# Region and embedding gathers in overlapping fours, and a reordered set-up, in a two-layer LSTM kernel

## What is computed

```python
rp = jnp.concatenate([region_tbl[region_idx], poi_tbl[poi_idx]], -1)
nv = jnp.concatenate([rp @ W_rp + b_rp, coords @ W_co + b_co], -1)
conv = jax.nn.elu(lax.conv_general_dilated(nv, conv_w, (1,), 'VALID', ...) + conv_b)
emb = jnp.tanh(jnp.concatenate([car_tbl[car_idx], week_tbl[week_idx], time_tbl[time_idx]], -1))
x = jnp.concatenate([conv, jnp.broadcast_to(emb[:, None, :], conv.shape[:2] + (27,))], -1)
h = _lstm_layer(x, Wih0, Whh0, bih0, bhh0)
h = _lstm_layer(h, Wih1, Whh1, bih1, bhh1)
return ((h[:, -1, :] @ W1 + b1) @ W2 + b2) @ W3 + b3
```

## Time and profile before

| | |
|---|---|
| median of 3 runs | 1105.63 us (1104.09 to 1105.67) |
| profiled execution | 1107.28 us, its span 1105.5 us |
| mean granted TensorE clock | 0.991 |
| PE busy | 1071.1 us (97%) |
| DVE busy | 741.9 us (67%) |
| ACT busy | 511.5 us (46%) |
| POOL busy | 319.6 us (29%) |
| HBM read, written | 11.21 MB, 4.19 MB |

### The profile page before, as it was taken

One profiled execution on the slowest core, in us unless ns is written; L12 is line 12 of the kernel. 1 busy time (PEld: TensorE's weight loads), 2 busy tenths in 40 slices (PEclk: granted clock), 3 DMA queues, 4 the chain that ended last, 5 costly groups with the idle time before them and its releaser, 6 DMA issues.

```text
span 1105.5 us, 14346 instructions
## 1 busy us (share of the span) xinstructions
PE 1071.1 (97%) x4898; PEld 515.5 (47%) x4898; DVE 741.9 (67%) x1146; ACT 511.5 (46%) x737; POOL 319.6 (29%) x339
## 2 busy tenths in 40 slices
PE   5879999999999999999999999999999999999998
PEld 4654444444445444444444444444444544444444
DVE  3667766657777757567676858666686768766553
ACT  1354554444554544444554544444455544444432
POOL 3563045552440034552450025562541000000000
PEclk8979999999999999999999999999999999999999
DMA  9611001000010101000010101000010101000001
GB/s 240 135 14 16 1 3 31 2 2 1 2 31 2 39 3 31 3 2 1 2 31 1 41 2 31 3 2 1 2 31 1 39 1 27 3 0 1 1 1 38
DMA packets 36808, 22.57 MB, mean 20 GB/s; under 512 B 25303, under 2 KB 29447, under 8 KB 36615
## 3 DMA queue, kind: packets, MB, share of 16 engines
q1 hardware_dynamic: 24432, 20.53, 6.8%
q0 software_dynamic: 9984, 1.12, 2.6%
q10 hardware_dynamic: 2327, 0.08, 0.2%
HBM read 11.21 MB, written 4.19 MB: 14 GB/s over the span
## 4 chain that ended last, share of the span: by engine, by line
PE 85%; DVE 5%; issue 3%; DMA 2%; SPq 2%; ACT 2%; POOL 1%; DVEq 0%; ACTq 0%; POOLq 0%
PE acc L1311 49%; PE acc L1302 25%; PE acc L1293 5%; SPq L428 2%; PE aux L1400 2%; DMA feat<-in_L_rec_region_tbl,region_idx 2%; PE acc L1222 1%; POOL feat L549 1%; DVE neg_part L971 1%; PE aux L1163 1%; ACT gates L727 1%; PE aux L1257 1%; DVE h_full L1046 1%; DVE h_part L1047 1%; DVE gates L999 1%
## 5 line engine op out<-in xcount | busy, mean ns | idle before, releaser
L1311 PE MATMUL acc<-h_part,wh 128*128 128x512 f16 (+1 forms) x2688 | 656.0, 380 | 1.6 <-DVE h_part L1050 1.6
L1311 PEld LDWEIGHTS acc<-h_part,wh 128*128 128x128 f16 x2688 | 245.2, 98 | 321.6 <-issue 54.9
L1302 PE MATMUL acc<-h_part,wh 128*128 128x512 f16 (+1 forms) x1488 | 358.5, 379 | 0.0
L727 ACT ACTIVATE gates<-acc,gate_bias,unscale 128x512 f32<-128x512 f32 x254 | 195.9, 777 | 317.9 <-PE acc L1311 279.5
L727 ACT ACTIVATE gates<-gates,gate_bias,unscale 128x512 f32<-128x512 f32 x242 | 189.9, 811 | 152.4 <-DVE gates L999 142.4
L1302 PEld LDWEIGHTS acc<-h_part,wh 128*128 128x128 f16 x1488 | 144.5, 98 | 177.4 <-issue 6.2
L549 POOL DMA_INDIRECT feat<-in_L_rec_region_tbl,region_idx x160 | 161.9, 1012 | 182.8 <-PE acc L1311 127.7
L999 DVE TENSOR_TENSOR gates<-acc,emb_gates 128x512 f32<-128x512 f32 x242 | 161.3, 686 | 53.5 <-PE acc L1311 45.5
L549 POOL DMA_INDIRECT feat<-in_L_rec_poi_tbl,poi_idx x120 | 120.2, 1002 | 117.2 <-PE acc L1311 99.6
L1293 PE MATMUL acc<-x_in,wx 96*128 96x512 f32 (+1 forms) x248 | 137.3, 560 | 7.3 <-DMA x_in<-conv_hi 4.8
L1046 DVE TENSOR_TENSOR h_full<-gates,tanh_c 128x512 f32<-128x512 f32 x120 | 82.6, 689 | 75.8 <-ACT tanh_c L732 71.2
(11 more groups left out here) (135 smaller groups left out, 358.5 us busy)
## 6 DMA issues: line engine op xcount, KB each, us to landing
out<-y SPq DMA_DIRECT2D x16, 256.0 KB, 2.1
x_in<-conv_hi SPq DMA_DIRECT2D x56, 64.0 KB
feat<-in_L_rec_region_tbl,region_idx POOLq DMA_INDIRECT x160
w<-in_L_rec_W SPq DMA_DIRECT2D x2, 1024.0 KB, 9.3
w_nat<-in_L_rec_Whh SPq DMA_DIRECT2D x2, 1024.0 KB
w<-in_L_rec_W SPq DMA_DIRECT2D x1, 2048.0 KB
feat<-in_L_rec_poi_tbl,poi_idx POOLq DMA_INDIRECT x120
x_in<-conv_lo SPq DMA_DIRECT2D x28, 64.0 KB
```

The source lines that it names most:

```text
L727: nc.scalar.activation(gates[layer][:, j, g, :], source, ACT.Tanh if g == GATE_G else ACT.Sigmoid, bias=gate_bias[:, layer, m:m + 1], scal ...
L1302: mm = nc.tensor.matmul(bank, wh[:, 1, a, c, rows], h_part[0][:, s.write_slot, b, c, :], start=(c == 0 and a == b == HI), stop=(s.first an ...
L1311: mm = nc.tensor.matmul(bank, wh[:, own_w, a, c, rows], h_part[layer][:, s.read_slot, b, c, :], start=False, stop=(c == HK - 1 and a == LO))
```

## The change

- **Gathers of chunk 0.** POOL starts as soon as the small indices are there with the embeddings' first four (car and time for two groups), then step 0's region four; the embeddings' second four once the first has landed; step 1 once step 0 has landed; step 2 once the second embedding four has; step 3 once step 1 has. Two semaphores (`rows_first_in[0]`, `[1]`) are used in turn. At most eight gathers are under way. The copy of the embeddings follows at once. The coordinates of chunk 0 are copied by ACT (`coords_first_put`).
- **Loads.** Whh0 comes before `poi_all`, which is loaded in eight pieces (`POI_PIECES`); W3 comes after Wih1 and Whh1; the week table goes to ACT's queue. The biases and b2 are loaded as rows of 128 (`bias_nat`, ACT's queue), transposed by PE (`turn_biases`) and added by DVE out of `aux` (`add_biases`).
- **Order.** PE multiplies the first four blocks of W1 W2 ahead of the projection's transpose and the band; `turn_wh(2)` and the embeddings' gates come before the first cell; the second half of `product_head` comes between the first and the second cell. DVE looks up the week first, makes the one-hot after the scales, and `row_maxima(1)` after `put_wx_lo`. The head's bias is summed in one piece between the fourth and the fifth cell, into a bank of `aux`, and `b_head` is made after the fifth cell.
- **Loop.** The first three cells of a chunk's body, (1,0), (0,2) and (1,1), stand at the end of the body before it (`early_cells`), and for chunk 0 in the set-up. Their order is the same.
- **Embeddings.** ACT writes `emb_in` with a second Tanh from the source, instead of DVE copying it.

```diff
+POI_PIECES = 4
...
-    return first, second
+    return (first, second) + early_cells(base, steps - 1)
+
+
+def early_cells(base, last_t):
+
+    bank = 14 % 4
+    return (make_cell(base, 1, 0, bank, (0, base.tile(2)), last_t),
+            make_cell(base, 0, 2, (bank + 6) % 4, (1, base.tile(1)), last_t),
+            make_cell(base, 1, 1, (bank + 6) % 4, (0, base.tile(3)), last_t))
...
-        bank = 14 % 4
-        yield cell(base, 1, 0, bank, (0, base.tile(2)))
-        bank = (bank + 6) % 4
-        yield cell(base, 0, 2, bank, (1, base.tile(1)))
-        yield cell(base, 1, 1, bank, (0, base.tile(3)))
+        bank = (14 + 6) % 4
...
+        if following:
+            for early in early_cells(after, last_t):
+                yield "cell", early
...
-        WH_BANKS = ((0, 1, 2, 1), (2, 1, 0, 3), (3, 1, 0, 2))
+        WH_BANKS = ((0, 1, 2, 1), (2, 0, 1, 3), (2, 0, 1, 3))
...
+            load(w_nat[0][:, :, :], d["Whh0"].rearrange("(m p) k -> p m k", p=P), w_in[0])
+
             poi_rows_of = d["r_poi_idx"][0:NCOL, :].rearrange("(s b) t -> s (b t)", s=SIDES)
+            piece = NCOL // SIDES * T // POI_PIECES
             for side in range(SIDES):
-                load(poi_all[side * POI:(side + 1) * POI, :, :].rearrange("k b t -> k (b t)"),
-                     poi_rows_of[side:side + 1, :].partition_broadcast(POI)[:, 0, :], poi_all_in)
-            load(w_nat[0][:, :, :], d["Whh0"].rearrange("(m p) k -> p m k", p=P), w_in[0])
+                for i in range(POI_PIECES):
+                    cols = slice(i * piece, (i + 1) * piece)
+                    load(poi_all[side * POI:(side + 1) * POI, :, :].rearrange("k b t -> k (b t)")[:, cols],
+                         poi_rows_of[side:side + 1, cols].partition_broadcast(POI)[:, 0, :], poi_all_in)
             load(wx_nat[:, :, 0:D_X], d["Wih0"].rearrange("(m p) k -> p m k", p=P), wx_in)
             coord_rows = d["r_coords"].rearrange("(g p) t c -> p g (t c)", p=P)
             load(coords[:, 0:GR, :], coord_rows[:, 0:GR, :], coords_in)
-            load(week_tbl[:, :, :].rearrange("p w d -> p (w d)"),
-                 d["week_tbl"].rearrange("(a w) d -> a (w d)", a=1).partition_broadcast(P)[:, 0, :], week_tbl_in)
-            load(w3[:, :, :], d["W3"].rearrange("(k p) n -> p k n", p=P), w3_in)
-            for layer in range(2):
-                for i, k in enumerate(("bih", "bhh")):
-                    load(bias_in[:, layer, i, :], d[f"{k}{layer}"].rearrange("(m p) -> p m", p=P), bias_loaded)
             for i, k in ((1, "Wih1"), (2, "Whh1")):
                 load(w_nat[i][:, :, :], d[k].rearrange("(m p) k -> p m k", p=P), w_in[i])
+            load(w3[:, :, :], d["W3"].rearrange("(k p) n -> p k n", p=P), w3_in)
...
+                    pool.wait_ge(small_put, 1)
+                    gather_emb(0, 2)
                     pool.wait_ge(idx_ready, 1)
-                    for t in range(PAIR_WIN):
-                        gather_steps(t, t + 1, False, rows_first_in)
-                        pool.wait_ge(rows_first_in, (t + 1) * GR * DMA)
-                    pool.wait_ge(coords_in, DMA)
-                    copy_coords()
-                    pool.wait_ge(small_put, 1)
-                    for g in range(0, GR, 2):
-                        gather_emb(g, g + 2)
-                        pool.wait_ge(emb_rows_in, (g + 2) * (2 * DMA))
+                    gather_steps(0, 1, False, rows_first_in[0])
+                    pool.wait_ge(emb_rows_in, 2 * 2 * DMA)
+                    gather_emb(2, 4)
+                    pool.wait_ge(rows_first_in[0], GR * DMA)
+                    gather_steps(1, 2, False, rows_first_in[1])
+                    pool.wait_ge(emb_rows_in, 4 * 2 * DMA)
+                    gather_steps(2, 3, False, rows_first_in[0])
+                    pool.wait_ge(rows_first_in[1], GR * DMA)
+                    gather_steps(3, 4, False, rows_first_in[1])
...
-            load(b2_col[:, :], d["b2"].rearrange("(k p) -> p k", p=P), b2_in)
+            load(week_tbl[:, :, :].rearrange("p w d -> p (w d)"),
+                 d["week_tbl"].rearrange("(a w) d -> a (w d)", a=1).partition_broadcast(P)[:, 0, :], week_tbl_in)
+            for layer in range(2):
+                for i, k in enumerate(("bih", "bhh")):
+                    row = (layer * 2 + i) * M
+                    load(bias_nat[row:row + M, :], d[f"{k}{layer}"].rearrange("(m p) -> m p", p=P), bias_loaded)
+            load(bias_nat[4 * M:BIASES, :], d["b2"].rearrange("(k p) -> k p", p=P), bias_loaded)
...
+                nc.scalar.activation(emb_in[:, :], source, ACT.Tanh).then_inc(emb_step, 1)
...
+            for m in range(4):
+                put_w12(m)
             put_proj()
-            for m in range(K2):
+            for m in range(4, K2):
                 put_w12(m)
             act.wait_ge(wx_in, DMA)
             for k, first_col, copies, width in ((0, 0, 3, D_CONV), (3, D_CONV, 4, D_EMB)):
                 nc.scalar.copy(wx_rep[:, :, k:k + copies, 0:width],
                                wx_nat[:, :, first_col:first_col + width].unsqueeze(2)
                                .to_broadcast([P, M, copies, width])).then_inc(wx_copied, 1)
+            act.wait_ge(coords_in, DMA)
+            nc.scalar.copy(feat[:, :, :, D_REG + D_POI:D_FEAT],
+                           coords[:, 0:GR, :].rearrange("p g (t c) -> p g t c", c=2)).then_inc(coords_first_put, 1)
...
-            put_head_hi(1)
             emb_tanhs(0, acc[:, 0, :])
             put_wh_hi(1)
-            act.wait_ge(bias_ready, 1)
-            first, second = opening_cells(STEPS)
-            cell_acts(first)
+            put_wh_hi(2)
             for part in range(3):
                 put_emb_gates(0, part)
-            put_wh_hi(2)
+            act.wait_ge(bias_ready, 1)
+            first, *others = opening_cells(STEPS)
+            cell_acts(first)
             put_turned(feat_t[0:KP, 1, :], acc[0:KP, 0, :], turned[0], 1, turned_put[0])
+            put_head_hi(1)
             elu_parts(1, slice(0, HALF))
-            cell_acts(second)
+            for s in others:
+                cell_acts(s)
...
+            def add_biases():
+                dve.wait_ge(bias_turned, 1)
+                bias = aux[:, 3, 0:4 * M].rearrange("p (l i m) -> p l i m", l=2, i=2)
+                nc.vector.tensor_copy(gate_bias[:, :, :], bias[:, :, 0, :]).then_inc(bias_step, 1)
+                nc.vector.tensor_copy(b2_col[:, :], aux[:, 3, 4 * M:BIASES]).then_inc(b2_put, 1)
+                dve.wait_ge(bias_step, 1)
+                nc.vector.tensor_tensor(gate_bias[:, :, :], gate_bias[:, :, :], bias[:, :, 1, :], ALU.add
+                                        ).then_inc(bias_ready, 1)
...
-                nc.vector.tensor_copy(emb_in[:, :], emb_tanh[:, :]).then_inc(emb_step, 1)
...
+            week_lookup()
+            poi_parts()
+            add_biases()
+            row_maxima(0)
+            row_scales(0)
+            poi_one_hot()
             put_band()
             put_conv_bias()
-            poi_parts()
-            poi_one_hot()
-            row_maxima(0)
-            row_scales(0)
-            week_lookup()
             put_poi()
             put_wx_lo()
-            add_head_bias()
+            row_maxima(1)
             put_wh_lo(0)
-            dve.wait_ge(bias_loaded, 4 * DMA)
-            nc.vector.tensor_tensor(gate_bias[:, :, :], bias_in[:, :, 0, :], bias_in[:, :, 1, :],
-                                    ALU.add).then_inc(bias_ready, 1)
-            elu(0, slice(0, HALF), (0, slice(0, HALF)), ())
-            sum_head_bias(0, K2 // 2)
-            put_head_lo(0)
-            row_maxima(1)
             row_maxima(2)
             row_scales(1)
-            put_head_lo(1)
+            elu(0, slice(0, HALF), (0, slice(0, HALF)), ())
+            put_head_lo(0)
+            add_head_bias()
             split_emb(0)
             put_wh_lo(1)
-            first, second = opening_cells(STEPS)
+            put_wh_lo(2)
+            first, second, third, fourth, fifth = opening_cells(STEPS)
             cell(first)
-            sum_head_bias(K2 // 2, K2)
-            put_wh_lo(2)
+            put_head_lo(1)
             elu(1, slice(0, HALF), (0, slice(HALF, NCOL)), ())
-            dve.wait_ge(head_bias_acc, 1)
-            dve.wait_ge(b3_in, DMA)
-            nc.vector.tensor_tensor(b_head[:, :], acc[:, 1, :], b3_row[:, :], ALU.add).then_inc(head_bias_put, 1)
             cell(second)
             dve.wait_ge(x_second_put, HALVES_DMAS * DMA)
             later = slice(GR, NB * GR)
             indices(1, "region", REG, later, (later_idx_in, 2 * DMA))
+            cell(third)
+            cell(fourth)
+            sum_head_bias()
             dve.wait_ge(idx_ready, 2)
             indices(2, "poi", POI, later, (later_idx_in, 2 * DMA))
+            cell(fifth)
+            dve.wait_ge(head_bias_acc, 1)
+            dve.wait_ge(b3_in, DMA)
```

(58 more changed lines are left out.)

34 lines of the change are left out of this document (18 added, 16 removed).

## The result

The changed kernel took 1103.47 us (median of 20 runs) beside 1105.70 us of the kernel before: a ratio of 0.9982, 95% interval 0.9974 to 0.9990. So 2.2 us were gained where 4.6 had been forecast (1101.0, range 1096 to 1106). One of the 20 executions took 1602.81 us at a mean granted clock of 0.656, and the ratio leaves it out.

| set | kernel before, median | changed kernel, median | ratio, 95% interval |
|---|---|---|---|
| result | 1105.70 | 1103.47 | 0.9982 [0.9974, 0.9990] |
| A | 1106.68 | 1110.89 | 1.0045 [1.0024, 1.0066] |
| B | 1107.21 | 1111.29 | 1.0040 [1.0026, 1.0054] |
| C | 1106.86 | 1102.97 | 0.9974 [0.9956, 0.9992] |
| D | 1105.98 | 1102.91 | 0.9973 [0.9962, 0.9984] |

The account below looks back on a forecast made before the run. PE is full from about 102 us, so gains must come before the second cell at 88.1. Set-up 4.7 plus b_head's wait 0.84 less bias matmuls 0.9 gives 4.6: 1105.63 to 1101.0 us, range 1096.0 to 1106.0.

Parts of the forecast that it names:

- The product W1 W2 and turn_wx: Set-up on PE: product starts at 13.2 after 3.5 us more of ACT's issues; turn_wx at 34.1, bounds 33.2 to 36.5.
- The gathers ... land at 38.5 to 42: in time for 42.2: POOL's 24 first gathers: last issued by 36.3, about 5.5 us a landing, before the first steps' turn at 42.2.
- Rival 4: Gather issues stretch beside DVE to 1.63 us each with the gap: last landing 47.2, kernel 1106.0; chance 0.04.
- Rival 3: Gathers bound by their number, 2.6 us each under load: first steps turn 11.7 us later, kernel 1115.7; chance 0.10.
- 7.5 us a landing: Slow end for the gathers: the last region rows would land at 44 and 1.5 us would be lost.
- rival 5: First steps still wait for gathers, only the loads' order gains: upper part of the forecast's own range, no separate chance.
- The order ahead of that turn: DVE's row_maxima(1) before put_wh_lo(0) sets the first steps' turn: 34.1 + 5.1 + 2.3 + 0.7 = 42.2.
- The head's product: Its first half starts on PE at 44.2 instead of 47.32: 3.1 us gained, bounds 0 and 4.
- From there to the second cell: Head's product to second cell on PE: second cell at 83.4 against 88.13, 4.7 us gained in all, bounds 80 to 86.5.
- a time at 1.2 GHz: Added to the head's second half, 7.0 us on PE before the second cell: 1.7 us for a halved clock.
- Behind it: After the second cell starts: b_head's wait gone (-0.84), head bias' two matmuls added (+0.9), DVE's head_sum costed at nothing.
- The loop's edge: Three early cells move across the loop's edge in unchanged order; on a full PE this costs nothing.

Follow-up runs that it names:

- quarter_w12: Changed kernel with only the first of four steps of W1*W2's product made (head's result wrong): 1102.67 us, 0.3 us from the control.
- region_first: Changed kernel with the four region fours issued ahead of the embeddings' fours: 1105.33 us (0.9998 of the kernel before), and 1106.22 us (0.9985) on another chip.
- set E: Two variants of the changed kernel on one chip: region rows first, 1106.22 us (0.9985); five eighths of the head's first product in the wait, 1107.90 us (1.0014).
- no_emb_rows: Changed kernel without the eight embedding gathers of the first batch, their columns zeroed: 1099.65 us, 0.9939 of the kernel before.
- pool_pause: Changed kernel with GpSimd waiting for the third quarter of Whh0 before the last eight region gathers: 1110.28 us, 7.31 us over the control.

## Why the prediction was wrong

The forecast was 4.7 us for the set-up and next to nothing behind it; the medians give 2.2 in all. In the traces the set-up gave 2.5 (the second cell at 85.6 instead of 88.1). The step that failed is the gathers: the region rows were to land before DVE was through, and they landed after it. The steps in turn:

- **The product W1 W2 and turn_wx: right, on the careful side.** Forecast 13.2 and 34.1, measured 11.68 and 31.66. ACT's five further issues and that of b2, which was there before, took 2.9 us (7.57 to 10.51), and the product started 2.0 us later than before, where I had counted 3.5; the clock was full from 12 us on. quarter_w12 shows that none of this reached the end.
- **"The gathers ... land at 38.5 to 42: in time for 42.2": the step that failed.** The last was issued at 42.6 instead of 36.3, and the turn came at 43.96. Three sizes were off. The first gather went at 7.09 instead of 5.9. The first four landed 20.41 - 11.93 = 8.5 us behind its last issue, where I had taken 5.5 out of rows of 5.6 to 7.5; together the third four went at 20.4 instead of 16. And three gathers beside DVE's one-hot took 2.07, 1.85 and 1.23 us instead of 0.94, 2.3 us more. (Rival 4 was this at a size for all 24. Rival 3, 2.6 us a gather, didn't come: from 7.09 to 42.59 the 24 were issued 1.48 us apart on the mean. The Trainium skill, SBUF — State Buffer, SBUF: two separate sides, says that a DVE instruction in a mode that takes both of its ports keeps GpSimd from writing descriptors. The row of the gather at 25.41 agrees: it ended at 27.48, 0.1 us behind DVE's tensor_scalar of 25.82 to 27.37. In which mode that instruction ran, no row shows.) The other end of my bound, 7.5 us a landing, was in the text with its consequence: landing at 44, 1.5 us lost (44 against 42.2 is 1.8). The turn came at 43.96, but that the number fits is in part luck: only the first landing was that slow, a later one (step 1's, 32.42 to 37.9) took 5.5 us as I had assumed, and the rest of the delay is the late start and the stretched issues. By its mechanism this is rival 5, the gathers still what the first steps wait for; I had given it no chance of its own and put it at the upper part of my range, up to 1103.4.
- **The order ahead of that turn** I had right in one thing and wrong in its weight: DVE was through at 39.8, the turn's other condition, so by its rows the turn could have come 2.4 us ahead of the forecast. region_first shows DVE as the releaser once the rows are early, though with late copies, so no run shows the turn at 39.8. I had compared a forecast of 42.2 on one side with 42 on the other and called it "in time".
- **The head's product** came at 47.20 instead of 44.2: 1.8 us from the turn, and 1.2 since the turn, a quarter of Whh0 and the convolution ran at 1.2 GHz (1.03, 1.92), where I had taken 2.0 for them as before. After standing still for 5.9 us PE paid again behind the wait.
- **From there to the second cell** 38.4 us against 39.2 forecast, and 2.63 us of idle PE before turn_wh(1) against 2.7. The sum is right partly by luck: up to the second turn (77.65) it took 1.0 us more than forecast, and behind it 1.8 less, because the head's second half ran in 7.03 us, so that the 1.7 for a time at 1.2 GHz never came. Of the 3.0 lost, 0.8 came back here.
- **Behind it:** no wait for b_head, as forecast. DVE's head_sum from 125.75 to 131.7 delayed no matmul: PE waited 1.3 us in all between 90 and 180, none of it there. The loop's edge "costs nothing": within what can be told, yes. But 0.84 gained and 0.9 lost should have left the rest of the span as it was, and it was 1.8 us shorter in set D and 2.5 in the first two traces. A good part of the 5.0 us by which those two differ was not forecast, and why ACT's gates and x_in hold PE up less stays open.

DVE's rows of head_sum, with what stands behind them:

```profile
125.75 0.48 DVE L939 TENSOR_SCALAR head_sum<-w,b 128x512 f32<-128x512 f32 x1
126.27 5.47 DVE L943 SCALAR_TENSOR_TENSOR head_sum<-w,b,head_sum 128x512 f32<-128x512 f32 x7
131.66 0.21 DVE L823 TENSOR_SCALAR idx_wrap<-poi_raw 128x120 f32<-128x120 int32 x1
```

The range held the time in three of the five sets. In the other two the case that took over was on no list of mine: ScalarE gets TensorE's results of the stretch from 36 to 50 us late, by 3 to 10 us. What is shown of it: it appeared in sets A, B and E and in no trace of sets C and D or of the result; it comes with the granted clock full or half, and with TensorE's waits filled or not. In set A it was absent from the kernel that issues its gathers one four at a time and short in the one with the region rows first, and in set E too the kernel with the region rows first had none while the one with the changed order (and part of the head's product in the wait) had, so that the order of the gathers may have a part in it; these are single traces, though in set A the medians (1106.1 and 1105.3 against 1110.9) point the same way. The kernel before was not traced on a chip that shows it. Its cause is not settled. One page would fit: the Trainium skill, TensorE: Matmul & The Clock Gate, Seeing it yourself, says that the clock's events in a trace have been unreliable on trn2, and that the clock has been seen held at a quarter for over 50 us. An estimate from that page's quarter: a quarter of Whh0, 0.89 us at full, would take 3.6 us. The runs show 2.9 and 4.25, so it agrees in direction and not in size.

## What to carry over

A wait that is to vanish has two conditions behind it; forecast both, and where they come within 2 us of one another take the slow end of the less certain one. For a gather behind full queues that is the landing, which took 5.5 us once and 8.5 us another time in the same trace, and DVE's large instructions beside its issue count too. A control belongs into every set: the same kernel was 3.9 us faster than its predecessor on one chip and 4 us slower on another. And where a median moves, look in the trace for the stretch in which it moved: in set B it was not the one that the experiment had changed.

## What the runs showed of the hardware

- ScalarE's copies of TensorE's results came up to 9.5 us behind the modelled end of the matmul (turn_wh(0) in set A: modelled 39.92, last copy 49.45), mostly 2.9 or 4.25 us apart where 0.89 is usual, at a granted clock of 1.00 (set E, 41 to 50 us) and of 0.50 (set A, 45 to 50 us) alike.
- A four of gathers of 128 rows landed 4.7 to 9.0 us behind its last issue with the DMA engines full (4.7 in region_first, 10.8 to 15.5; 9.0 in no_emb_rows, 12.15 to 21.11; DMA share 0.84 to 1.2), and 1.4 us behind it with them nearly empty (42.6 to 44.0; share 0.07).
- The issue of a gather, 0.94 us, took 1.2 to 2.6 us beside DVE's one-hot (2.58 in pool_pause); with the one-hot in pieces, 1.1 to 1.8.
- In a wait of 5.9 us on TensorE (38.1 to 44.0) the granted clock fell at 43.3 and stayed at 1.2 GHz until 46.7, which made 1.2 us more of the next three steps. More work put into the wait held the clock (35.2 to 48.9 us) on a chip with late copies, and won nothing by it there.
